# First attention: one weight tile per head copied inside SBUF, keys interleaved over the tiles, and two products moved to the end of the next head

## The reference, cut to what matters

```
C = S // SPLIT                                    # 1024 // 64 = 16 chunks
scores = einsum('bhqd,bhckd->bhcqk', q, kc) * scale
w = softmax(scores.astype(float32), axis=-1)      # over the 64 keys of a chunk
chunk_out = einsum('bhcqk,bhckd->bhcqd', w, vc)
sum_w = w.sum(axis=-1, keepdims=True)
combined = (chunk_out * sum_w).sum(axis=2)        # over the chunks
out = combined / (sum_w.sum(axis=2) + 1e-09)
```

## Time and profile before

| | |
|---|---|
| median of three runs | 2207.07 us |
| the profiled execution | 2210.59 us |
| its span on the core | 2208.5 us |
| PE busy | 1976.8 us (90%) |
| DVE busy | 1440.1 us (65%) |
| ACT busy | 980.7 us (44%) |
| DMA packets | 187.99 MB |
| first attention of batch 0 | from about 23 to 534 us |
| first attention of batch 1 | from about 1112 to 1620 us |

### The profile page before, as it was taken

The page is one execution under the profiler, slowest core; times in us unless marked ns, Lnnn a source line. Parts: engine busy times, 40 slices in busy tenths (PEclk is TensorE's granted clock), DMA queues, the critical chain, the costliest instruction groups (busy, mean ns, idle before and its releaser), DMA issues.

```text
span 2208.5 us, 32078 instructions
## 1 busy us (share of the span) xinstructions
PE 1976.8 (90%) x10106; PEld 1193.3 (54%) x10106; DVE 1440.1 (65%) x2492; ACT 980.7 (44%) x1377; POOL 586.5 (27%) x549
## 2 busy tenths in 40 slices
PE   6899999996997999998888999999979889999985
PEld 4444444444784655556644444444448755655554
DVE  7677788865327777753467887778561377777443
ACT  3444454441224666662334444444413246656422
POOL 0000000000101798884120000000010047897921
PEclk7999999998887999998879999999979879999987
DMA  2366665567000000000516565656750000000024
GB/s 94 84 154 160 155 149 141 139 161 237 24 1 10 2 10 6 1 1 30 163 39 154 141 146 141 146 141 151 182 198 1 1 10 10 1 6 1 1 79 135
DMA packets 84846, 187.99 MB, mean 85 GB/s; under 512 B 17697, under 2 KB 46754, under 8 KB 83106
## 3 DMA queue, kind: packets, MB, share of 16 engines
q1 hardware_dynamic: 83650, 183.76, 32.8%
q0 software_dynamic: 1024, 2.10, 0.3%
HBM read 178.47 MB, written 8.91 MB: 85 GB/s over the span
## 4 chain that ended last, share of the span: by engine, by line
PE 67%; DVE 14%; issue 9%; ACT 3%; DMA 3%; POOL 2%; SPq 1%; DVEq 0%; another core or an unknown queue 0%; POOLq 0%; ACTq 0%
PE PS L814 10%; PE PS L786 5%; PE PS L750 5%; PE PS L986 4%; PE PS L926 4%; PE PS L966 3%; DVE mx L1919 3%; PE PS L881 3%; PE PS L969 3%; PE PS L1159 3%; PE PS L771 3%; PE PS L776 3%; PE PS L1218 2%; DMA V<-weight_rows 2%; POOL Esum L2463 2%
## 5 line engine op out<-in xcount | busy, mean ns | idle before, releaser
L1919 DVE TENSOR_REDUCE mx<-PS 128x8 f32<-128x512 f32 x512 | 329.6, 686 | 178.7 <-PE PS L750 164.0
L2463 POOL TENSOR_TENSOR Esum<-Esum,EE 128x512 f32<-128x512 f32 (+3 forms) x320 | 341.3, 1094 | 15.5 <-POOL Esum L2463 10.5
L1948 DVE TENSOR_TENSOR EE<-EE,V 128x1024 f32<-128x1024 f32 x256 | 303.1, 1219 | 45.3 <-DMA V<-weight_rows 44.7
L1502 ACT ACTIVATE EE<-PS 128x1024 f32<-128x1024 f32 x256 | 259.9, 1024 | 142.7 <-PE PS L776 141.2
L2052 DVE TENSOR_REDUCE mrow<-PS 128x1 f32<-128x512 f32 (+3 forms) x384 | 204.1, 552 | 99.1 <-PE PS L929 69.9
L2405 POOL TENSOR_TENSOR QA<-hT,QA 128x512 fp32r<-128x512 f32 x2 | 2.6, 1282 | 996.5 <-ACT hT L1690 996.5
L814 PE MATMUL PS<-EE,Vlater 128*64 128x512 f32 x1024 | 250.5, 609 | 9.4 <-ACT U L1468 8.3
L750 PE MATMUL PS<-KA,QA 128*128 128x512 f32 x512 | 204.1, 454 | 31.8 <-DVE mx L1919 25.8
L1586 ACT ACTIVATE EE<-PS 128x1024 f32<-128x1024 f32 (+2 forms) x192 | 138.1, 739 | 121.4 <-PE PS L969 118.7
L771 PE MATMUL PS<-QA,KA 128*128 128x512 f32 x512 | 185.1, 443 | 0.0
L750 PEld LDWEIGHTS PS<-KA,QA 128*128 128x128 f32 x512 | 97.8, 196 | 130.3 <-DVE mx L1919 88.4
(11 more groups left out here) (321 smaller groups left out, 3373.6 us busy)
## 6 DMA issues: line engine op xcount, KB each, us to landing
V<-weight_rows SPq DMA_DIRECT2D x512, 256.0 KB, 5.4
EE<-in_w SPq DMA_DIRECT2D x48, 192.0 KB, 2.7
V<-in_Wg SPq DMA_DIRECT2D x4, 1024.0 KB, 6.4
EE<-in_Wu SPq DMA_DIRECT2D x4, 1024.0 KB, 11.8
EE<-in_Wd SPq DMA_DIRECT2D x4, 1024.0 KB, 13.5
sorted_out<-U SPq DMA_DIRECT2D x12, 256.0 KB, 3.1
wo<-in_wo SPq DMA_DIRECT2D x5, 512.0 KB, 4.4
wq_s<-in_wq SPq DMA_DIRECT2D x17, 128.0 KB, 2.8
```

The lines of the kernel that those rows point to most:

```text
L1502: act.activation(EE[i % 2][:, t, :], banks(2 * (t % 2)), ACT.Exp, scale=QSCALE).then_inc(s["p2_exp"], 1)
L1919: dve.tensor_reduce(mx[:, t, half * 8:half * 8 + 8], banks(5 + x % 2, BANK).rearrange("p (c k) -> p c k", c=8), AX, ALU.max).then_inc(s["p ...
L1948: dve.tensor_tensor(EE[i % 2][:, t, :], EE[i % 2][:, t, :], weight_ring[a % 2][:, odd, :], ALU.mult).then_inc(p3_mul, 1)
L2463: ins = pool.tensor_tensor(Esum[:, h, lo:hi], Esum[:, h, lo:hi], e_tile(t)[:, h, lo - t * P:hi - t * P], ALU.add)
```

## The change

The keys of a group are dealt over the tiles: place k of tile t holds the key 8k + t. Each tile then holds eight keys of every one of the 16 chunks, and partition p of any tile belongs to chunk p // 8. So one weight tile of 128 x 1024 serves all eight tiles of a head.

- `project_k` and `project_v` read `att_in` through a view with a step of 8 elements (32 bytes) between neighbours, as moving operand and as weight operand.
- The keys of a chunk are now 8 places in each of 8 tiles. L750 reads KA in eight runs of 64, and the reduction on DVE goes over two axes: runs of 8 columns, 64 apart.
- `chunk_sums` takes one tile at a time: four matmuls of 256 queries per tile (32 a head) in place of 16 of 512, all with the same 0/1 matrix. The sums fill 256 columns in place of 512; the copies on ACT are 256 wide, and two transposes stand where four stood, at both places.
- No scratch in DRAM: four DMAs of 128 KB a head go from `r_rows` to one of two weight tiles in SBUF. All products of a head wait for the four of them.
- DVE's products: tiles 4 and 5 of head i - 1 stand at the end of head i, tiles 6 and 7 of head i - 2 at t = 1, and none at t = 3. PE's order of `values0` is as it was.

```diff
-                        def weight_rows_out(i):
+                        def weights_in(i):
                             sp.wait_ge(s_rr, b * HEADS + i + 1)
+                            if i >= 2:
+                                sp.wait_ge(p3_mul, 1 + (b * HEADS + i - 1) * NT)
                             for j in range(4):
-                                sp.dma_start(weight_rows[i % 2, odd * CQ:(odd + 1) * CQ, half * BANK:(half + 1) * BANK],
-                                             r_rows[32 * j:32 * j + CQ, :]).then_inc(wr_in, 16)
-                        def weight_tiles_in(i, a):
-                            for odd in range(2):
-                                t = 2 * a + odd
-                                if i >= 1 or t >= 4:
-                                    sp.wait_ge(p3_mul, 1 + (b * HEADS + i) * NT + t - 3)
-                                for k in range(2):
-                                    row = weight_rows[i % 2, odd * CQ + 2 * a + k, :]
-                                    sp.dma_start(weight_ring[a % 2][HD * k:HD * k + HD, odd, :],
-                                                 row.partition_broadcast(HD)).then_inc(wt_in[t % 4], 16)
+                                rows = r_rows[32 * j:32 * j + NC, :]
+                                sp.dma_start(weights[i % 2][:, j * QUARTER:(j + 1) * QUARTER],
+                                             rows.unsqueeze(1).to_broadcast([NC, CP, QUARTER])).then_inc(wt_in, 16)
...
+                by_place = x_in[:, :].rearrange("p (k t) -> p t k", t=NT)
...
-                    pe.matmul(banks(bank, BANK), wk_s[:, 0, :], x_in[:, half * BANK:(half + 1) * BANK],
+                    pe.matmul(banks(bank, BANK), wk_s[:, 0, :], by_place[:, :, half * HD:(half + 1) * HD],
...
-                        mm = pe.matmul(banks(bank, HD, t * HD), x_in[:, t * P:(t + 1) * P], wv_s[:, 0:HD],
+                        mm = pe.matmul(banks(bank, HD, t * HD), by_place[:, t, :], wv_s[:, 0:HD],
...
-                def chunk_sums(i, a):
-                    pe.wait_ge(s["p2_exp"], 1 + (h0 + i) * NT + 2 * a + 2)
-                    for half in range(2):
-                        for odd in range(2):
-                            j = 2 * half + odd
-                            mm = pe.matmul(PS[32 * j:32 * j + 32, 4 * BANK:5 * BANK], chunk_sum[:, a, :],
-                                           EE[i % 2][:, 2 * a + odd, half * BANK:(half + 1) * BANK],
-                                           start=(a == 0), stop=(a == 3))
+                def chunk_sums(i, t):
+                    pe.wait_ge(s["p2_exp"], 1 + (h0 + i) * NT + t + 1)
+                    for j in range(4):
+                        mm = pe.matmul(PS[32 * j:32 * j + 32, 4 * BANK:4 * BANK + QUARTER], chunk_sum,
+                                       EE[i % 2][:, t, j * QUARTER:(j + 1) * QUARTER], start=(t == 0), stop=(t == NT - 1))
...
-                    for k in range(4):
+                    for k in range(2):
                         mm = pe.transpose(banks(4, P, k * P), S_sb[:, k * P:(k + 1) * P], ident)
...
-                    act.activation(r_rows[:, :], banks(4, BANK), ACT.Copy).then_inc(s_rr, 1)
+                    act.activation(r_rows[:, :], banks(4, QUARTER), ACT.Copy).then_inc(s_rr, 1)
...
-                                          banks(5 + x % 2, BANK).rearrange("p (c k) -> p c k", c=8),
-                                          AX, ALU.max).then_inc(s["p1_max"], 1)
+                                          banks(5 + x % 2, BANK).rearrange("p (t c k) -> p c t k", t=NT, k=CP),
+                                          AXY, ALU.max).then_inc(s["p1_max"], 1)
...
-                            if t % 2 and t < 5 and i >= 2:
-                                weigh(i - 2, t + 3 + k)
+                            if t == 1 and i >= 2:
+                                weigh(i - 2, 6 + k)
...
+                    if i >= 1:
+                        for t in range(4, 6):
+                            weigh(i - 1, t)
                     if i + 2 < HEADS:
                         maxima(i + 2, UNITS_FIRST)
```

More of the change, by code:

```diff
@@ L13 @@
 AX = mybir.AxisListType.X
+AXY = mybir.AxisListType.XY
 ds = bass.ds
@@ L139, in layer_program @@
         Vlater = sb("Vlater", [P, NT - 2, 2, P])
-        weight_ring = [v[:, :, :].rearrange("p t d -> p (t d)").rearrange("p (o q) -> p o q", o=2) for v in V1]
+        weights = [V1[0][:, 4 * i:4 * i + 4, :].rearrange("p t d -> p (t d)") for i in range(2)]
         own0 = Vlater[:, :, :, :].rearrange("p t h d -> p (t h d)")
@@ L362, in layer_program @@
         s_rr = sem("s_rr")
-        wr_in = sem("wr_in")
-        wt_in = [sem(f"wt_in{i}") for i in range(4)]
+        wt_in = sem("wt_in")
         p3_mul = sem("p3_mul")
@@ L2003, in attention0 @@
                 normaliser_parts(step)
-                for t in range(4, NT):
+                for t in range(6, NT):
                     weigh(i - 1, t)
```

92 lines of the change are left out of this document (44 added, 48 removed).

## The result

The changed kernel takes 2222.12 us (median of 20 runs, 2210.35 to 2229.22), the kernel before 2205.6 us beside it (median of 20, 2198.62 to 2214.0). The ratio is 1.0072, with a 95% interval from 1.0059 to 1.0085: slower by 16.5 us between the medians, where 2221 and +13.5 were forecast. The same kernel in a later set (e11) gave 1.0066. The profiled execution of the changed kernel took 2214.05 us, with a span of 2212.1, and so is one of its shortest. Set beside the profile of before it shows 3.5 us only; where most of the others are stands under the experiments, at e7 and e12.

The account below looks back on a forecast made before the run. PE, 93% busy in the first attention, was taken as the bound, with DVE's chain pacing part of each head. -2.2 - 1.3 - 2.9 + 19.9 = +13.5 us on 2210.6; against the median, 2221 us, 8-in-10 range 2188 to 2243.

Parts of the forecast that it names:

- the likeliest case: The forecast itself: stepped reads slow PE's projections as they slowed DVE, 2221 us, own range 2212 to 2231, chance 0.37.
- Moved products: DVE's pair of products, 2.35 us, leaves t = 3 for idle time ahead of the first maxima: value 0.
- Transposes and copies: Fewer transposes, narrower copies: about 0.08 us in each of 28 heads, 2.2 us, plus 1.3 us in the last two heads.
- DMA path: Scratch traffic hidden except in each batch's tail, where PE reaches the output product 1.5 us earlier: 2.9 us gained in all.
- Chunk sums: 64 matmuls of 256 columns cost no more than 32 of 512: 0 taken, at most 6 us in all.
- Reductions over two axes: DVE's reductions of 512 columns in PSUM, read in runs of 8, take as long as before: value 0.
- Keys with a step: PE's keys' projection takes 0.85 us more a call; twelve calls in the heads at t = 3 and t = 5: +10.2 us.
- Values with a step: PE's stepped weight loads take 214 ns instead of 113, 1.6 us more a call; six calls at t = 3: +9.7 us.
- the rival of a read in each cycle: In the projections PE reads SBUF every cycle, so a stepped keys' call costs 2.55 us more: 2241 us, chance 0.10.
- that of free steps: Stepped reads in PE's projections hide behind two-cycle columns and cost nothing: 2201 us, chance 0.27.
- The calls at the start: Four stepped keys' calls at the start of a batch cost nothing, as a column takes as long anyway at the lower clock.
- signs that were named for a right reading: Expected trace marks, among them values' loads of 3.4 us and DVE waiting for weights only at the last head's products.

Follow-up runs that it names:

- e11: The changed kernel unchanged, measured once more in a later set: 1.0066 of the kernel before.
- e7: Changed kernel with the values' projection split into two halves, tiles 0 to 3 at step 3 and 4 to 7 at step 5, both stepped: 1.0010 of the kernel before.
- e12: Second measurement of the changed kernel with the values' projection in two stepped halves: 1.0021 of the kernel before.
- e4: Changed kernel with the earlier order of weighings, tiles 4 and 5 at step 1, 6 and 7 at step 3: 1.0056 of the kernel before.
- e5: Changed kernel with four transposes and copies of 512 columns as before, in place of two and 256: 1.0099 of the kernel before.
- e6: Changed kernel with each head's weights sent twice, first into an unread buffer, and both awaited: 1.0144 of the kernel before.
- e1: Changed kernel with the keys' projection reading in one run, keys placed by stepped PSUM reads on ACT and DVE: 2212.36 us, 1.0015 of the kernel before.

## Why the prediction was right

The sum came out within 3 us of the measured difference, and the likeliest case was the one that happened: stepped reads on PE cost about what a stepped read cost DVE. That part is understanding. That the sum is so close is in part luck, since its terms erred on both sides. In the stretches that the change touches, the two profiles differ by +13.7 (heads), -2.7 (tails) and +1.9 (starts), 12.9 in all. With the profile of e11 it is +12.2, +0.4 and +2.0, 14.6 in all.

- *Moved products, 0.* Right for the middle heads, by e4. What the move is worth at the end of a batch, about 1.1 us, the forecast had in its term for the DMA path.
- *Transposes and copies, -2.2 and -1.3.* Right in mechanism for the first pair (the stall grew, 0.64 to 1.08) and for the last heads (22.31 to 21.69, -0.62 each against -0.65). Too small in between: "only about 0.08 us can be had" because the reductions at 341.35 start when the products end. "PE's values at t = 3 wait for the second of these" is the reading that was wrong: PE's groups behind the second transposes don't wait for them, so 0.17 to 0.21 a head is kept. By e5, heads and tails together, the term is some 6 to 7 us rather than 3.5.
- *DMA path, -2.9, in the tail alone.* The tails are -2.7, but e5 gives 1.4 of them to the transposes and e4 1.6 to the moved products, which leaves nothing for the path itself, and in e11 the lower clock takes all of it back (50.3 and 50.4 us). So the closeness of this number is luck. The step that failed is "before the last two heads the DMA path is hidden": a wait of 2.3 us in four pieces was read as nothing, while it stood in head 1 and PE waited 3.1 us behind it. Without the stepped keys head 1 is 24.20 us in both batches, 2.15 less than in batch 1 of before (26.35; batch 0 has 27.94, with 3.4 us at the lower clock). The transposes make 0.2 of it by e5 and the order nothing by e4; that the rest is the earlier weights is what remains, and e6 shows the same place from the other side.
- *Chunk sums, 0.* Right: 3.66 us for 64 records, 3.64 for 32.
- *Reductions over two axes, 0.* Right, 685 and 686 ns.
- *Keys with a step, +10.2.* 0.95 a call against 0.85. Both ends of that difference were low: by the starts of its records a column takes 0.53 us / 512 = 1.04 ns in one run, where 0.85 was read, and 0.98 / 512 = 1.92 ns with the step, where 1.67 was taken. In the heads 4 x 1.9 and 2 x 1.0 (head 1, where part of a call is covered) make 9.7.
- *Values with a step, +9.7.* 2.0 a call against 1.6 makes 12.1, and behind it the clock, which the forecast didn't have: 1.3 us for about every second call, 3 to 4 us (two to five of six calls in a profile). A load's 0.24 us for 128 columns is 1.86 ns a column where DVE's stepped element, 1.67 ns, was taken over. So the rival of a read in each cycle falls, and so does that of free steps.
- *The calls at the start, nothing.* Wrong for batch 0. "The four at the start of a batch fall in a stretch at the lower clock": the profile of the changed kernel has the full clock from 27 to 33 us, and that of the kernel before has it from 27 to 30 us, so that this could have been read beforehand. There stand

```profile
27.20 2.00 PE L671 MATMUL PS<-att_in,wk_s 128*128 128x512 f32 x2
...
29.03 3.78 PE L677 MATMUL PS<-wv_s,att_in 128*128 128x64 f32 x16
...
32.62 0.80 PE L740 MATMUL PS<-KA,QA 128*128 128x512 f32 x2
```

By the starts the second call of the keys takes 1.83 us and the values 3.59; before it was 0.86 and 2.49 (with 0.60 of waiting for an eviction in it). The first sums come 3.1 us later. In batch 1 the profiles show no such loss (34.6 against 35.8 us).

Of the signs that were named for a right reading two were off: the loads took 3.8 us and not 3.4, and DVE waits 6.7 us for the weights of the last head but one too (at 498.74 us in batch 0), not for those of the last alone. Heads with a projection of queries changed by 0.17 us, where more than 0.3 would have been wrong.

So about 7 us of gains were missed (head 1, the second transposes) and about 8 us of losses (longer loads, their clock, the starts). Had one side alone been missed, the time would have been 7 or 8 us off the forecast.

On the rule about lines of 16 bytes in "SBUF — State Buffer" of the Trainium skill, section "Door 1: The DMA port swizzle": PE's moving read at a step of 32 bytes took 0.98 us for 512 columns where it takes 0.53 in one run, which agrees in direction. For PSUM, e1 shows no such cost when ACT and DVE read it with the same step.

## What to carry to other kernels

A layout that another stage wants was cheapest here where an engine takes a result out of PSUM: the step that lengthened PE's reads of SBUF by 85% (moving) and 110% (weights) was free there. A wait of 1 us is to be looked up by its place before it is called small, above all in the first and last rounds of a loop, which have less cover than the middle ones. And of two profiles whose difference is under 1%, the stretches that the change can't touch are compared first: here one of them moved by 10 us. The times of the single executions help as well: where they fall into groups, a profile shows one group only.

## What was not expected of the hardware

- The granted clock fell to its lower level behind 3.8 us of stepped weight loads with 64-column matmuls, 19 times in 36 in the heads, and not once in 12 when these were cut into two pieces of 1.9 us with other matmuls between them.
- ACT's and DVE's reads of PSUM in steps of eight fp32 elements cost nothing (597 and 676 ns, 596 and 676 in one run), while DVE's read of SBUF with a step of 16 elements in the earlier trace rows took 367 against 286.
- An unchanged stage took 127 or 137 us, at a mean granted clock of 0.91 or 0.83 to 0.85, within one execution, and the course could be told from whether the clock rose 13.4 to 13.7 or 14.0 to 15.6 us after the stage began (28 stretches, no exception).
- GpSimd's copy of 128x1024 took 1.03 us in one run, and 2.00 us in batch 1 (2.23 in batch 0) for another tile of this size that it read with the step.
